# Last rows of a layer norm on VectorE, unread products on TensorE, one column of gelu on ScalarE, and a VectorE step one column later in a recurrence

## The chip, the cores and the metric

One core of a Trainium2 chip runs the whole program in one launch. Its engines are TensorE (matrix products, the profile's PE, with PEld for its weight loads), VectorE (DVE), ScalarE (ACT), GpSimd (POOL) and SyncE (SP), which only issues transfers here. The metric is the device time in microseconds of one execution, lower is better; the median of several executions is compared.

## The reference

A decoder layer of three blocks over x of 2 x 1024 tokens by 256, each followed by a layer norm without weights. All is float32.

```python
# 1 gated linear attention: 16 heads, keys of 8, values of 16; h is 8 x 16 per head
gk = log_sigmoid(x @ Wgk1 @ Wgk2 + bgk2) / 16
h  = h * exp(gt)[..., None] + kt[..., None] * vt[..., None, :]     # 1024 steps
ot = einsum('bhk,bhkv->bhv', qt * scale, h)
o  = o * rsqrt(mean(o * o) + eps) * gnw * (g * sigmoid(g))
x  = layernorm(x + o @ Wo)
# 2 cross attention over 64 of 64 context rows picked by index, 16 heads, latent of 128
x  = layernorm(x + softmax(q k / 4) v @ W_out.T)
# 3 pre-norm causal attention, and 8 gelu experts of 1024, the two best per token
a   = attention(ln(x)) @ Wo + bo + x
mid = gelu(einsum('bsd,edf->bsef', ln2(a), e_w1) + e_b1)
x   = layernorm(x + sum_e w_e * (mid @ e_w2 + e_b2) + a)
```

## The kernel before

The program is written out by hand: each engine has its own list of instructions in each of four program blocks, and semaphores tie them together. There is no scheduler; the order in which a method is called in an engine's function is the order of execution. Tokens are handled in four tiles of 512 (NB = 4), m or k in the code. Between two program blocks all engines meet.

**Block 1, the recurrence** (`front`). The state is kept as 32 columns jj (2 batches x 16 values), each a scan along 1024 steps with 128 rows of head and key. For each column VectorE does `state` (the scan, line 526), perhaps an extra step, `product(jj + 1)` (value times key, line 521) and `output(jj)` (state times query, line 531). TensorE works two columns ahead: `values(jj + 2)` spreads the value row over 128 partitions (line 307), `sums` (line 314) and `turn` (line 320) bring four columns at a time back to tokens. The projections for the second batch are fitted between them: tile 3's x is turned (line 114), ScalarE copies its high part (`x_hi`, line 651), VectorE subtracts it to get the low part (`x_lo`, line 505), TensorE forms the low-rank gate input (`low`, line 263, with Wlp), ScalarE copies it (line 749), TensorE forms the gate (line 273), ScalarE goes through Identity, Abs, Exp and Ln (lines 659 to 667), and VectorE's `log_sigmoid(1)` (line 511) reads it after column 11. ScalarE also makes 0/1 rows for counting indices (`signs`, line 696), which TensorE adds up (line 335).

**Block 2, the cross attention** (`cross_blocks`). It first finishes block 1's output for tiles 2 and 3: product with Wo, statistics on VectorE, and `out_rows` on ScalarE (line 886), which reads y from PSUM (banks G2 = 4, 5 and G3 = 6, 7) and writes normed rows to X. Then for each tile m TensorE runs `exps(m, 0)` (scores again, transposed, lines 1120 and 1124), `c_q` (queries of tile m + 1, line 1005), `values(m, 0)` (lines 1137 and 1140, into banks 6 and 7), `exps(m, 1)`, `scores(m + 1, ...)` (lines 1094 and 1099), `values(m, 1)` and `wout` (line 122). ScalarE takes the exponentials (line 1217), VectorE the maxima (line 1289), the reciprocals of the sums (line 1296) and the quotients (line 1298). `wout` waits for the last quotient.

**Block 3, the causal attention** (`attend`): eight groups g of four heads; TensorE's order goes by steps c of two score banks each; the units of the next group's row maxima (`units`) stand between them, into banks 0 to 3. At c = 16 the maxima are turned. In group 6 (NG - 2) no units follow after c = 14. The last group's order holds the router's first steps: `turn_sums`, `project`, `turn_normed`, `logits`. `warm(n, bank)` (line 1876) issues n products of the identity that nothing reads.

**Block 4, the experts** (`moe`): 256 steps s of one expert's 128 hidden values for 512 tokens. TensorE does a first layer (line 2467) and, three steps later, a second layer (line 2480); ScalarE takes the gelu (line 2549), VectorE splits it in a high and a low part (lines 2614 and 2616). In the first steps expert 0's second-layer weights are also split, the high part on ScalarE (line 2214), the low part on VectorE (line 2219).

## Time and profile before

| | |
|---|---|
| median of three executions | 1375.2 us (1374.62 to 1379.39) |
| the profiled execution | 1377.79 us, of which the span from first to last instruction is 1376.1 us |
| PE busy | 1292.6 us (94% of the span) |
| DVE busy | 978.4 us (71%) |
| ACT busy | 643.9 us (47%) |
| POOL busy | 140.2 us (10%) |
| mean granted TensorE clock | 0.975 of full |

A share of busy time is a mean over four blocks with different limits, so the blocks are read apart. In a list of instructions in order of time, the number ahead of the engine's name is the duration of a group, and the bracket at a row's end is how long the engine sat idle before it and what ended that. A clock of 1.00 is 2.4 GHz and 0.50 is 1.2 GHz. A PE row's duration holds some time of the last product's way through the array, so two neighbouring PE rows overlap a little.

### The profile page before, as it was taken

What the parts mean: (1) busy time and instruction counts of PE and PEld (TensorE: products, weight loads), DVE (VectorE), ACT (ScalarE), POOL (GpSimd) and SP (SyncE); (2) the same over time, 40 slices, a digit from 0 to 9 for tenths busy, and PEclk for the clock granted to TensorE, in tenths of its full rate; (3) what the DMA queues carried; (4) which work ended last, traced back from release to release, by engine and by line L of the source; (5) the groups of instructions that cost most, each with busy time, mean ns of one, the idle gap of its engine ahead of it and who ended that gap; (6) DMA issues with size and microseconds to landing.
All of it is one profiled execution on the core that took longest, in us unless ns stands there. A gap on an engine that the chain in (4) does not pass through costs nothing.

```text
span 1376.1 us, 19007 instructions
## 1 busy us (share of the span) xinstructions
PE 1292.6 (94%) x7577; PEld 954.3 (69%) x7577; DVE 978.4 (71%) x1409; ACT 643.9 (47%) x944; POOL 140.2 (10%) x220
## 2 busy tenths in 40 slices
PE   8786868999899999999999999999999999999997
PEld 7454536567655555557788888888888888888886
DVE  6899996898699898846775655655546556555566
ACT  5677664336468777874433423323223223232233
POOL 5000003000514332210000000000000000000000
PEclk9899989999999999989999999999999999999999
DMA  4000001003522212113000012111101102010001
GB/s 139 1 0 1 0 1 35 1 1 117 171 90 59 64 53 58 55 32 108 16 1 17 4 39 66 48 38 31 57 13 47 39 16 69 16 39 16 1 16 46
DMA packets 40329, 55.78 MB, mean 41 GB/s; under 512 B 9553, under 2 KB 26625, under 8 KB 40241
## 3 DMA queue, kind: packets, MB, share of 16 engines
q1 hardware_dynamic: 35056, 43.67, 10.5%
q0 software_dynamic: 3648, 10.09, 2.6%
q8 instruction: 60, 0.98, 0.3%
q10 hardware_dynamic: 1536, 0.81, 0.2%
q14 instruction: 29, 0.23, 0.1%
HBM read 43.73 MB, written 10.55 MB: 39 GB/s over the span
## 4 chain that ended last, share of the span: by engine, by line
PE 52%; DVE 2%; ACT 1%; issue 0%; ACTq 0%; DVEq 0%
PE PS L2467 25%; PE PS L2480 24%; PE PS L122 1%; PE PS L114 0%; PE PS L2493 0%; PE PS L2228 0%; PE PS L2253 0%; DVE OT_all L2623 0%; DVE r_st L2307 0%; DVE r_on L2324 0%; DVE r_on L2304 0%; PE PS L2505 0%; DVE X L2316 0%; DVE x_mid L2614 0%; ACT X L2586 0%
## 5 line engine op out<-in xcount | busy, mean ns | idle before, releaser
L2549 ACT ACTIVATE x_g<-PS,x_bias 128x512 f32<-128x512 f32 x256 | 175.9, 687 | 494.3 <-PE PS L2467 493.8
L2467 PE MATMUL PS<-x_h,x_w 128*128 128x512 f32 x1536 | 401.1, 396 | 0.5 <-ACT x_g L2549 0.5
L2480 PE MATMUL PS<-x_mid,x_w 128*128 128x512 f32 x1488 | 383.9, 393 | 1.2 <-DVE x_w L2219 1.2
L2467 PEld LDWEIGHTS PS<-x_h,x_w 128*128 128x128 f32 x1536 | 286.9, 188 | 66.1 <-ACT x_g L2549 1.4
L2480 PEld LDWEIGHTS PS<-x_mid,x_w 128*128 128x128 f32 x1488 | 279.2, 188 | 66.0 <-DVE x_w L2219 1.7
L2614 DVE CAST x_mid<-x_g 128x512 fp32r<-128x512 f32 x256 | 109.3, 427 | 275.5 <-ACT x_g L2549 275.3
L2088 DVE TENSOR_REDUCE a_M<-PS 128x2 f32<-128x1024 f32 (+1 forms) x144 | 173.1, 1224 | 26.0 <-PE PS L1792 19.9
L2616 DVE TENSOR_TENSOR x_mid<-x_g,x_mid 128x512 fp32r<-128x512 f32 x256 | 177.2, 692 | 8.8
L2028 ACT ACTIVATE f_parts<-PS 128x512 f32<-128x512 f32 x224 | 120.7, 601 | 36.7 <-PE PS L1846 24.9
L1869 PE MATMUL PS<-f_parts,aV 128*32 128x256 f32 (+1 forms) x960 | 75.9, 398 | 0.2 <-POOL f_parts L1680 0.2
L696 ACT ACTIVATE c_hot<-c_idxT,c_cid 128x1024 bf16<-128x1024 bf16 x65 | 70.7, 1139 | 5.2 <-PE PS L337 3.9
L526 DVE TENSOR_TENSOR_SCAN qh<-decay,qh 128x1024 f32<-128x1024 f32 x32 | 73.0, 2283 | 0.0
L2447 POOL DMA_DIRECT2D x_wb<-route_w x31 | 16.7, 539 | 476.9 <-DVE OT_all L2623 453.2
L1846 PE MATMUL PS<-aQ,aK 64*128 64x512 f32 x192 | 51.0, 488 | 0.7 <-ACT f_h L2028 0.7
L1846 PEld LDWEIGHTS PS<-aQ,aK 64*128 64x128 f32 x192 | 20.4, 184 | 37.8 <-ACT f_parts L2028 27.0
L2623 DVE SCALAR_TENSOR_TENSOR OT_all<-PS,x_bias,x_wb 128x512 f32<-128x512 f32 x62 | 46.2, 745 | 0.0
L1680 POOL TENSOR_SCALAR_AFFINE_SELECT f_parts<-f_parts 128x512 f32<-128x512 f32 x45 | 28.6, 634 | 163.9 <-ACT f_parts L2028 144.4
L307 PE MATMUL PS<-vparts,g_sel 128*128 128x512 f32 x128 | 39.9, 437 | 5.3 <-DVE qh L521 4.6
L1788 PE MATMUL PS<-aK,aQ 64*128 64x512 f32 (+3 forms) x256 | 36.7, 331 | 7.0 <-PEq L1052 2.7
L2219 DVE TENSOR_TENSOR x_w<-x_raw,x_w 128x1024 fp32r<-128x1024 f32 x32 | 38.9, 1219 | 1.4 <-ACT x_w L2214 1.4
L521 DVE TENSOR_TENSOR qh<-PS,KT 128x1024 f32<-128x1024 f32 x32 | 38.6, 1207 | 1.3 <-PE PS L314 1.2
L531 DVE TENSOR_TENSOR qh<-qh,QT 128x1024 f32<-128x1024 f32 x32 | 38.9, 1216 | 0.0
(371 smaller groups left out, 1589.2 us busy)
## 6 DMA issues: line engine op xcount, KB each, us to landing
x_raw<-L_ffn_e_w SPq DMA_DIRECT2D x32, 512.0 KB, 3.8
qk_parts<-f_parts SPq DMA_DIRECT2D x16, 512.0 KB, 3.6
x_wb<-route_w POOLq DMA_DIRECT2D x31, 256.0 KB, 3.4
aQ<-qk_parts SPq DMA_DIRECT2D x96, 64.0 KB, 2.6
aK<-qk_parts SPq DMA_DIRECT2D x60, 64.0 KB, 2.8
X<-x SPq DMA_DIRECT2D x4, 512.0 KB, 7.6
aK<-qk_parts SPq DMA_DIRECT2D x36, 48.0 KB, 2.0
out<-X SPq DMA_DIRECT2D x3, 512.0 KB, 2.9
```

The source lines that it names most:

```text
L526: e.tensor_tensor_scan(qh[:, jj % RQ, :], decay[:, batch(jj // HD)], qh[:, jj % RQ, :], 0.0, ALU.mult, ALU.add).then_inc(s_h, 1)
L696: e.activation(hot[:, n % RS, :], self.idxT[:, :], ACT.Sign, bias=self.cid[:, c:c + 1], scale=2.0).then_inc(s_sg, 1)
L1846: last = e.matmul(bank, K[q][R, s, tile(TB * h if kind == "k0" else kind)], Q[q][R, s, q0:q0 + BLK], start=True, stop=True)
L1869: last = e.matmul(PS[32 * j:32 * j + 32, 7, dst:dst + w], Vs[m % 2][:, kt, j, :], x, start=k in (0, 3) and half == 0, stop=k in (2, NQD - ...
L2028: e.activation(buf[k][:, j, :], PS[:, 4 + b % 3, :], ACT.Exp).then_inc(A.sem, 1)
L2088: e.tensor_reduce(dst, src, AX.X, ALU.max, negate=True).then_inc(VC.sem, 1)
L2467: last = e.matmul(PS[:, f % 2, :], w1[n % 2][u][:, kt, f * P:(f + 1) * P], self.rows(v, k)[:, kt, :], start=m == 0 and kt == 0, stop=m == ...
L2480: last = e.matmul(PS[:, 2 + 2 * (it % 2) + d, :], w2[n % 2][v][:, f, d * P:(d + 1) * P], mid[u][:, f % RM, :], start=f == 0 and m == 0, st ...
L2549: e.activation(g[s % RG][:, :], PS[:, f % 2, :], ACT.Gelu, bias=b1[:, n, f:f + 1]).then_inc(A.sem, 1)
L2614: e.tensor_copy(mid[0][:, f % RM, :], g[s % RG][:, :]).then_inc(V.sem, 1)
L2616: e.tensor_tensor(mid[1][:, f % RM, :], g[s % RG][:, :], mid[0][:, f % RM, :].bitcast(F32), ALU.subtract).then_inc(V.sem, 1)
L2623: e.scalar_tensor_tensor(out=(y if n else sumT[k])[:, d, :], in0=PS[:, 2 + 2 * (it % 2) + d, :], scalar=b2[:, n, d:d + 1], in1=wb[:, it % ...
```

## The change

Five edits.

1. In the recurrence, VectorE's `x_lo(3, 4)` is called after the scan of column 7 instead of column 6.
2. The last normed rows of tile 3 are written by VectorE (`out_rows_vector`: subtract the mean, multiply by the reciprocal deviation) instead of ScalarE (`out_rows`); TensorE's first `values` waits for VectorE's new step "out".
3. In the cross attention, for m = 0, 1 and 2, four products of the identity, 128x512 each, stand ahead of `wout`. Nothing reads them.
4. In the causal attention's group 6, three such products stand at step c = 15 and three at c = 17 (bank 0, behind a wait for the last maximum that reads it), and three more in the last group ahead of `turn_normed`.
5. ScalarE computes the gelu of one column of 128 values behind the router's exponentials, at the end of block 3; nothing reads it.

```diff
@@ recurrence, VectorE @@
                     elif jj == 4:
                         x_lo(2, 4)
-                    elif jj == 6:
+                    elif jj == 7:
                         x_lo(3, 4)
@@ new method @@
+    def out_rows_vector(self, e, m, banks):
+        e.wait_ge(self.OV[m].sem, self.OV[m].at("nmr"))
+        for t in range(TB):
+            last = e.tensor_scalar(self.X[:, m * TB + t, :], self.PS[:, banks[t // 2], t % 2 * D:(t % 2 + 1) * D],
+                                   self.o_mv[m % 2][:, t, 0:1], self.o_rstd[m % 2][:, t:t + 1], ALU.subtract, ALU.mult)
+        last.then_inc(self.OV[m].sem, 1)
@@ cross attention, TensorE @@
-                        e.wait_ge(self.OA[3].sem, self.OA[3].at("out"))
+                        e.wait_ge(self.OV[3].sem, self.OV[3].at("out"))
...
                     scores(m + 1, 3)
+                    for _ in range(4):
+                        e.matmul(PS[:, EB[0], :].rearrange("p (c n) -> p c n", n=P), identr[:, :], identr[:, :].unsqueeze(1).broadcast_to((P, TB, P)), start=True, stop=True)
                     wout(m, range(TB - 1))
@@ cross attention, ScalarE @@
-                self.out_rows(e, 3, G3)
@@ cross attention, VectorE @@
                 self.out_rstd(e, 3)
+                self.out_rows_vector(e, 3, G3)
@@ causal attention, TensorE @@
+                        if g == NG - 2 and c in (15, 17):
+                            e.wait_ge(VC.sem, VC.at(f"c{NU - 2}", NG - 1))
+                            warm(3, SPARE)
...
                 quad_sums(NG - 1, 6)
+                warm(3, SPARE)
                 self.turn_normed(e, 0, FREE)
@@ causal attention, ScalarE @@
                 self.exps(e, 0)
+                e.activation(self.f_nmr[:, 0:1], self.eps[:, 0:1], ACT.Gelu)
                 sums_out(NG - 1, 1)
```

The lines of the changed kernel stand 6 to 16 higher than those of the kernel before. VectorE's order in the recurrence, columns 5 to 8 (minus is before, plus is after; line 505 is `x_lo(3)`):

```order
 L531 TENSOR_TENSOR qh<-qh,QT 128x1024
 L526 SCALAR_TENSOR_TENSOR qh<-decay,qh 128x1024
+L521 TENSOR_TENSOR qh<-PS,KT 128x1024
+L531 TENSOR_TENSOR qh<-qh,QT 128x1024
+L526 SCALAR_TENSOR_TENSOR qh<-decay,qh 128x1024
 L505 TENSOR_TENSOR XTp<-PS,XTp 128x2x512
-L521 TENSOR_TENSOR qh<-PS,KT 128x1024
-L531 TENSOR_TENSOR qh<-qh,QT 128x1024
-L526 SCALAR_TENSOR_TENSOR qh<-decay,qh 128x1024
 L521 TENSOR_TENSOR qh<-PS,KT 128x1024
 L531 TENSOR_TENSOR qh<-qh,QT 128x1024
```

One product, one output and one scan now stand ahead of the low part.

ScalarE's order at the start of the cross attention, before (line 886 is `out_rows`, 1217 the exponentials):

```order
L988 ACTIVATE vparts<-PS 128x512
L886 ACTIVATE X<-PS,go_nmr,go_rstd 128x256 x4
L144 ACTIVATE go_sd<-go_mv,eps 128x4
L886 ACTIVATE X<-PS,go_nmr,go_rstd 128x256 x4
L1217 ACT_TABLE_LOAD
L1217 ACTIVATE pr<-PS 128x512 x4
```

and after:

```order
L994 ACTIVATE vparts<-PS 128x512
L886 ACTIVATE X<-PS,go_nmr,go_rstd 128x256 x4
L144 ACTIVATE go_sd<-go_mv,eps 128x4
L1226 ACT_TABLE_LOAD
L1226 ACTIVATE pr<-PS 128x512 x4
```

The second set of four is gone from ScalarE; it stands on VectorE as `L893 TENSOR_SCALAR`, between the step that ends tile 3's statistics and the split of the queries. The table load now follows the square root.

ScalarE's order from the end of block 3 into block 4, before (line 2276 is the router's exponentials, 2009 the last sums out of PSUM, 2549 the gelu):

```order
L2276 ACTIVATE r_ex<-r_lg 128x32
L2009 ACTIVATE OT_all<-PS 128x512
L1643 UNCONDITIONAL_BRANCH
L2538 UNCONDITIONAL_BRANCH
L2551 ACTIVATE x_bias<-PS 128x80
L2549 ACT_TABLE_LOAD
L2549 ACTIVATE x_g<-PS,x_bias 128x512
```

and after:

```order
L2292 ACTIVATE r_ex<-r_lg 128x32
L2080 ACT_TABLE_LOAD
L2080 ACTIVATE f_nmr<-eps 128x1
L2023 ACTIVATE OT_all<-PS 128x512
L1652 UNCONDITIONAL_BRANCH
L2554 UNCONDITIONAL_BRANCH
L2567 ACTIVATE x_bias<-PS 128x80
L2565 ACTIVATE x_g<-PS,x_bias 128x512
```

The number of table loads stays the same; this one has moved from the front of the first gelu to behind the router's exponentials.

## Rows read from the trace of the kernel before

**Rows 1.** Busy time by stretch: length, then each engine, clock, DMA.

```profile
40.00:206.00 166.00, 125.67 (x708) 76.38 (x707) 158.97 (x138) 122.42 (x129) 0.00 (x0) 0.88 0.00 1
...
629.00:1376.00 747.00, 736.53 (x3332) 602.73 (x3332) 448.18 (x806) 233.61 (x323) 17.71 (x33) 1.00 0.11 34
```

**Rows 2.** Instructions in order of time, recurrence: start, us, engine, line, [idle before].

```profile
60.20 1.23 DVE L505 TENSOR_TENSOR XTp<-PS,XTp 128x1024 fp32r<-128x1024 f32 x1 [3.80 <-ACT XTp L651]
61.35 1.22 DVE L521 TENSOR_TENSOR qh<-PS,KT 128x1024 f32<-128x1024 f32 x1
61.48 2.95 PE L263 MATMUL PS<-XTp,Wlp 128*16 128x512 f32 x12 [1.36 <-DVE XTp L505]
...
65.27 1.00 ACT L749 ACTIVATE c_L<-PS 16x1024 f32<-16x1024 f32 x1
65.81 1.20 DVE L521 TENSOR_TENSOR qh<-PS,KT 128x1024 f32<-128x1024 f32 x1
...
66.32 1.98 PE L273 MATMUL PS<-c_L,Wgk 16*128 16x512 f32 x4 [0.20 <-ACT c_L L749]
```

**Rows 3.** The same, where VectorE meets ScalarE again.

```profile
82.38 1.06 ACT L667 ACTIVATE decay<-decay 128x1024 f32<-128x1024 f32 x1
83.60 1.20 DVE L511 SCALAR_TENSOR_TENSOR z<-z,decay 128x1024 f32<-128x1024 f32 x1
89.61 1.22 DVE L514 TENSOR_TENSOR vparts<-PS,vparts 128x1024 fp32r<-128x1024 f32 x1 [0.34 <-ACT vparts L681]
```

**Rows 4.** The same, start of the cross attention.

```profile
233.21 0.30 ACT L144 ACTIVATE go_sd<-go_mv,eps 128x4 f32<-128x4 f32 x1 [4.07 <-DVE go_mv L139]
233.95 1.93 ACT L886 ACTIVATE X<-PS,go_nmr,go_rstd 128x256 f32<-128x256 f32 x4 [0.45 <-DVE go_nmr L880]
233.97 2.89 PE L1005 MATMUL PS<-vparts,Wgp 128*128 128x512 f32 x12
235.90 1.28 ACT L1217 ACT_TABLE_LOAD   x1
236.90 0.69 DVE L1015 TENSOR_SCALAR qT_hi<-PS 128x512 fp32r<-128x512 f32 x1 [2.98 <-PE PS L1005]
237.20 2.06 ACT L1217 ACTIVATE pr<-PS 128x512 f32<-128x512 f32 x4
239.31 1.63 PE L1137 MATMUL PS<-pr,c_Vblk 128*32 128x512 f32 x8 [2.45 <-ACT pr L1217]
242.58 1.20 PE L1120 MATMUL PS<-vparts,XTp 32*128 32x512 f32 x12
```

**Rows 5.** Busy time in one microsecond of it.

```profile
241.00:242.00 1.00, 1.00 (x8) 0.00 (x0) 0.00 (x0) 0.00 (x0) 0.00 (x0) 0.50 0.00 0
```

**Rows 6.** The same two steps of TensorE for the next tile.

```profile
265.70 1.06 PE L1137 MATMUL PS<-pr,c_Vblk 128*32 128x512 f32 x8
...
267.55 0.74 PE L1120 MATMUL PS<-qT_hi,XTp 32*128 32x512 f32 x8
```

**Rows 7.** TensorE ahead of `wout`, in order of time.

```profile
255.02 2.86 PE L122 MATMUL PS<-c_WoutT,c_Kblk 128*128 128x256 f32 x12 [1.08 <-DVE c_Kblk L1298]
```

**Rows 8.** Line 492's fourteen unread products.

```profile
L492 PE MATMUL PS<-c_idr x14: 388/389/389, 203.3 to 206.3; 128*128 128x512 f32 x14
```

**Rows 9.** One microsecond near the end of the causal attention.

```profile
617.00:618.00 1.00, 1.00 (x2) 0.32 (x2) 0.00 (x0) 0.55 (x1) 0.00 (x0) 0.50 0.00 0
```

**Rows 10.** TensorE's idle time where products are added.

```profile
585.14 0.49 PE L1846 MATMUL PS<-aQ,aK 64*128 64x512 f32 x2 [0.67 <-ACT f_h L2028]
...
606.60 1.09 PE L114 MATMUL PS<-ident,r_on 128*128 128x128 f32 x8 [0.88 <-DVE r_on L2324]
```

**Rows 11.** From the causal attention's end into the experts.

```profile
616.95 0.60 ACT L2009 ACTIVATE OT_all<-PS 128x512 f32<-128x512 f32 x1 [2.80 <-PE PS L1869]
...
622.07 1.28 ACT L2549 ACT_TABLE_LOAD   x1 [2.49 <-PE PS L2467]
...
628.98 1.66 PE L2480 MATMUL PS<-x_mid,x_w 128*128 128x512 f32 x6 [1.22 <-DVE x_w L2219]
```

More of the change, by code:

```diff
@@ L822, in out_buffers @@
         self.OA = [self.steps(f"go_act{m}", ["sq", "sqrt", "ogT", "sd", "out"]) for m in range(NB)]
-        self.OV = [self.steps(f"go_dve{m}", ["ms", "rs", "norm", "gate", *self.NORM, "nmr"]) for m in range(NB)]
+        self.OV = [self.steps(f"go_dve{m}", ["ms", "rs", "norm", "gate", *self.NORM, "nmr", "out"]) for m in range(NB)]
         self.og, self.ogT = {}, {}
```

## The prediction

> **What bounds the kernel now.** I read the chain of waits first (nearly all of it is TensorE's two expert layers), then busy time by stretch, then each place that an edit touches in the list of instructions in order of time, looking at two things in a row: the bracket at its end (who was waited for) and the start against the end of the row it needs. Three limits follow one another. In the recurrence VectorE is busy 159.0 of 166.0 us [rows 1], so a wait of VectorE there looks like lost time. In the cross attention the engines hand work to each other and whatever releases TensorE's next step counts. In the experts TensorE is busy 736.5 of 747.0 us [rows 1]; there only what TensorE waits for at the very start can still be won, and everything won earlier is kept, since no later stretch waits for a fixed time.
>
> **Edit 1, the low part a column later.** VectorE idles 3.80 us ahead of `x_lo(3)`, until ScalarE has copied the high part [rows 2]. It was free at 60.20 - 3.80 = 56.40. Now a whole column goes first; from product to product a column takes 65.81 - 61.35 = 4.46 us, so the low part starts at 60.86 at the earliest, when its input is long there, and the 3.8 us of idling become work. That would be 3.80 us if VectorE stayed the limit. Two things speak against it. First, the low part itself comes 60.86 - 60.20 = 0.66 us later, and TensorE's `low` (61.48) was waiting for just it. ScalarE takes the result at 65.27 with nothing idle ahead of it, while `low` ended at about 64.4, so ScalarE does not notice; TensorE does, for its gate product at 66.32 had only 0.20 us of idle time ahead of it [rows 2]. The chain behind it is therefore late by 0.66 - 0.20 = 0.46 us at most, and by about 0.2 if the modelled end of the product before it is generous; I take 0.3. Second, VectorE needs this chain again: the Ln that `log_sigmoid(1)` reads ends at 82.38 + 1.06 = 83.44, and VectorE takes it at 83.60; the values' high part is waited for at 89.61 with 0.34 us idle [rows 3]. So VectorE had only 0.16 us of slack at 83.60 although it had lost 3.80 us before, and it can't come earlier than ScalarE. What it wins at 60 it waits at 83.6. Cost: +0.3 us; bounds +0.5 and, if the chain moved with VectorE after all, -3.8.
>
> **Edit 2, tile 3's rows.** ScalarE writes them from 233.95 to 235.88, loads the exponential's table (1.28 us) and exponentiates from 237.20 to 239.26; TensorE idles 2.45 us and starts `values` at 239.31, 0.05 behind [rows 4]. Without the rows ScalarE goes from the square root's end, 233.21 + 0.30 = 233.51, to the load, and is through with the exponentials at 233.51 + 0.02 + 1.28 + 2.06 = 236.87. TensorE's query product ends at 233.97 + 2.89 = 236.86, so `values` starts at 236.92: 2.39 us earlier. VectorE has the cover: it idles 2.98 us up to 236.90 [rows 4]. The trace has no such step on 256 columns out of PSUM; the nearest row is line 1015's on 512 columns, 0.69 us. Four steps cost between 4 x 0.35 and 4 x 0.69, 1.4 to 2.8 us, and end between 235.4 and 236.8 when started at 233.95: hidden at both ends, barely so at the upper. I take half the width, half the price. What is late next is TensorE's own query product.
>
> The idle 2.45 us had a second price. The granted clock behind it is 0.50, that is 1.2 GHz [rows 5], and from `values` to the next step (1137 to 1120) pass 242.58 - 239.31 = 3.27 us; for the next tile at full clock 267.55 - 265.70 = 1.85 us [rows 4, 6]. With the gap gone TensorE is busy throughout and I take the clock to stay at 2.4 GHz: another 1.4 us. TensorE stands idle next only ahead of `wout` (1.08 us, waiting for the quotient) [rows 7], and VectorE's reciprocals, which feed that, start on the end of `values`; so both parts arrive. Sum -3.8 us; bounds -2.4 (the clock falls anyway) and -4.1.
>
> **Edit 3, unread products ahead of `wout`.** Fourteen of the same form start between 203.3 and 206.3, (206.3 - 203.3) / 13 = 0.23 us each [rows 8]; four are 0.92 us against 1.08 us of idle time [rows 7]. They run instead of a wait: 0. At half clock they would be 1.84 us and cost 0.76 us, three times. The clock at these places is full now, so they also win nothing. 0, bounds 0 and +2.3.
>
> **Edit 4, nine more.** Three are 0.7 us. Ahead of `turn_normed` TensorE idles 0.88 us, hidden. Those at c = 17 stand before the last group's first scores; TensorE idles 0.67 us a little later, at 585.14 [rows 10], which takes them up at full clock; at half clock they are 1.4 us and cost 0.7. Those at c = 15 fall in a wait for ScalarE. If they keep the clock up that otherwise falls, as much comes back. 0, bounds -1.0 and +0.7.
>
> **Edit 5, gelu's table.** The load at 622.07 stands between TensorE's first layer and the first gelu. The second layer's first product, at 628.98, waited 1.22 us for the split of expert 0's weights on VectorE [rows 11], and the split waits for ScalarE, which does gelu, copy, gelu, copy in turn behind that load. So 1.28 us of load are 1.28 us of this chain. Ahead of 628.98 the second product of weights and both gelus only wait for ScalarE or have their products by then, so the whole comes through, and behind it TensorE is the limit. The new place is free: ScalarE idles 2.80 us ahead of 616.95 [rows 11], and load and one column are 1.28 + 0.25 us. -1.3 us; bounds 0 (a load that is still needed) and -1.5.
>
> The Trainium skill ("ScalarE: Activation LUTs", What ACT_TABLE_LOAD costs) gives such a switch 1.28 us and another 1.38 us for a drain, 2.66 us together. By that edit 5 would bring 2.7 us, and in edit 2 the exponentials would end later. The trace disagrees: from the load's start at 235.90 to the first exponential at 237.20 pass 1.30 us [rows 4].
>
> **The sum.** +0.3 - 3.8 + 0 + 0 - 1.3 = -4.8 us. The profiled execution took 1377.79 us, 1376.1 of span and 1.7 around it: 1373.0 us. It lies 2.6 us above the median 1375.2, and since the edits' terms don't depend on that, I take them from the median: 1370.4 us.
>
> **Rivals.** (a) VectorE is the limit of the recurrence after all, because the chain through ScalarE moves forward too: -3.8 instead of +0.3, so 1366.3 us. For it: 159.0 of 166.0 us busy [rows 1]. Against it: the slack of 0.16 us at 83.60 and the wait at 89.61 [rows 3]; the chain's next input from VectorE is the low part, and that comes later. (b) The unread products keep TensorE's clock up where it is 0.50 now, at the causal attention's end and the experts' start [rows 9]. Each microsecond at half clock in which TensorE is the limit gives back 0.5; were it 6 us of that kind (a guess at its length), 3 us, 1367.4 us. Against it: at 617 the clock is low, and the nearest added products stand ahead of 606.60, ten microseconds earlier, and fill only 0.7 us. (c) Slower: the first `values` now waits for VectorE's four steps. They decide from (236.87 - 233.95) / 4 = 0.73 us each; the whole change turns slower once they delay `values` past 239.31 by more than edits 5 and 1 leave, 1.0 us, that is from (239.26 + 1.0 - 233.95) / 4 = 1.6 us each. At 2.0 us each: 233.95 + 8.0 = 241.95, +2.7 us, less 1.0, so 1376.9 us. Against it: 0.69 us for twice the columns [rows 4]. (d) The clock falls at the same place all the same: 1.4 us less, 1371.8 us, and if the added products then run at half clock too, up to 3 us less, 1374.8 us.
>
> The Trainium skill ("TensorE: Matmul & The Clock Gate", Part 1) says that where the clock rises or falls varies from run to run of one kernel with the moment at which its products begin. No run here shows that yet; it would make (b) and (d) a matter of the run as much as of the change.
>
> **How the numbers follow.** Forecast 0.62; (a) 0.12; (b) 0.08; (c) 0.03; (d) 0.15. The forecast alone has 1369 to 1372 us. The range takes in (a) in part and the first half of (d): 1367.0 to 1373.8 us. What a measurement of this kernel tells from no change is 0.5%, 6.9 us, so faster is below 1368.3 us: (a), (b) and a little of the forecast, 0.20. Slower is above 1382.1 us: (c) at its far end, 0.03. The rest 0.77.
>
> **What would show it.** Edit 1: no idle time ahead of line 505, and instead two to four microseconds ahead of lines 521 and 511 between 75 and 84 us, with 511 at 83.7 to 84.0. Edit 2: `values` 0.1 us behind the query product, about 236.9, and a clock of 1.00 up to `exps`. Edit 3: no idle time left ahead of `wout`, and its start still on the quotient. Edit 5: no load at the first gelu, and the second layer's first product 5.6 us after ScalarE turns to the first gelu, where before it came 628.98 - 622.07 = 6.9 us after. I am wrong if VectorE enters column 12 over 1 us earlier than before, if the four steps end later than the exponentials, or if the experts' first second-layer product starts less than 1 us earlier against their first product.

## The result, and the profile after

| | before | after |
|---|---|---|
| median of the first comparison, us | 1375.35 (1374.18 to 1379.39, 6 runs) | 1367.91 (1365.43 to 1368.77, 6 runs) |
| ratio, 95% interval | | 0.9936 [0.9919, 0.9953] |
| ratio when measured again (f1 below) | | 0.9959 [0.9943, 0.9974] |
| mean of the runs that come with a clock, both sessions, us | 1374.88 (82 runs) | 1368.09 (12 runs) |
| mean granted clock of these runs | 0.9783 | 0.9810 |
| profiled execution, span, us | 1377.79, 1376.1 | 1367.98, 1366.2 |

The forecast was 1370.4 us, with no change beyond 0.5% as the likeliest outcome. The first ratio is 0.64% below one and clear of its uncertainty; over both sessions the means differ by 6.8 us, 0.49%. The gain is real and larger than the 4.8 us that the prediction summed, although the median of 1367.91 us lies inside its range of 1367.0 to 1373.8 us.

The profiled run of before lies 2.9 us above the mean of its kernel, that of after 0.1 us below it. So the 9.9 us between the two spans are more than the change brings, and the difference has to be split by place before any of it is credited to an edit. Busy time by stretch of the kernel after (length, then PE, PEld, DVE, ACT, POOL, granted clock, DMA share, GB/s):

```profile
40.00:206.00 166.00, 124.11 (x695) 73.88 (x694) 157.82 (x137) 122.58 (x129) 0.00 (x0) 0.88 0.00 1
629.00:1366.00 737.00, 726.70 (x3283) 594.46 (x3281) 440.30 (x792) 230.37 (x319) 17.22 (x32) 1.00 0.11 32
...
241.00:242.00 1.00, 1.00 (x5) 0.81 (x5) 1.00 (x1) 0.46 (x1) 0.00 (x0) 1.00 0.00 0
617.00:618.00 1.00, 1.00 (x5) 0.49 (x3) 0.96 (x3) 0.70 (x2) 0.57 (x1) 1.00 0.21 29
...
64.00:66.00 2.00, 2.00 (x6) 0.71 (x5) 2.00 (x3) 1.93 (x2) 0.00 (x0) 0.50 0.01 4
...
606.00:609.00 3.00, 3.00 (x22) 1.27 (x20) 1.97 (x12) 2.43 (x4) 0.83 (x2) 0.50 0.02 5
```

The same limits hold as in [rows 1]: VectorE in the recurrence, TensorE in the experts. The microseconds at 241 and 617, both at 0.50 before [rows 5, 9], are now at 1.00, that is 2.4 GHz. At 241 no stretch at half clock is left near. At 617 the comparison flatters: the change has moved the same work some 7 us earlier, and there 606 to 609 us is at 0.50. Before, half clock lasted from 611.7 to 622.0 us; now it lasts from 606.0 to 609.4 us. It is shorter, not gone.

The start of the cross attention after the change, in order of time, answers to [rows 4, 7]:

```profile
234.28 0.30 ACT L144 ACTIVATE go_sd<-go_mv,eps 128x4 f32<-128x4 f32 x1 [4.07 <-DVE go_mv L139]
234.60 1.28 ACT L1226 ACT_TABLE_LOAD   x1
235.03 1.90 DVE L893 TENSOR_SCALAR X<-PS,go_mv,go_rstd 128x256 f32<-128x256 f32 x4
235.90 2.06 ACT L1226 ACTIVATE pr<-PS 128x512 f32<-128x512 f32 x4
238.01 1.06 PE L1143 MATMUL PS<-pr,c_Vblk 128*32 128x512 f32 x8
239.87 0.97 PE L1126 MATMUL PS<-vparts,XTp 32*128 32x512 f32 x12
...
250.84 1.09 PE L1180 MATMUL PS<-c_idr 128*128 128x512 f32 x4
252.09 1.13 PE L122 MATMUL PS<-c_WoutT,c_Kblk 128*128 128x256 f32 x4 [0.16 <-DVE c_Kblk L1306]
```

The four rows on VectorE take 1.90 us together and end at 236.93, before the exponentials at 237.96. `values` (L1143) has no idle time ahead of it, and from it to the next step pass 239.87 - 238.01 = 1.86 us, against 3.27 before. From tile 3's square root to the output projection pass 252.09 - 234.28 = 17.81 us; before it was 255.02 - 233.21 = 21.81. That is edit 2, 4.0 us. The root itself comes 1.07 us later.

Further on, four rows of the kernel before (first units of the causal attention, turn of its first group, turn of its last, first product of the experts):

```profile
348.98 0.79 PE L1788 MATMUL PS<-aK,aQ 64*128 64x512 f32 x2 [2.73 <-PEq L1052]
...
386.53 0.67 PE L1817 MATMUL PS<-a_idr,a_nmp 128*128 128x128 f32 x5
...
579.91 0.77 PE L1817 MATMUL PS<-a_idr,a_nmp 128*128 128x128 f32 x5
...
618.93 0.37 PE L2507 MATMUL PS<-ident,r_eb 80*128 80x80 f32 x1 [0.90 <-PEq L1643]
```

And the same four of the kernel after, with ScalarE's gelu table and the second layer's first product, which answer to [rows 11]:

```profile
346.06 0.50 PE L1797 MATMUL PS<-aK,aQ 64*128 64x512 f32 x2 [2.70 <-PEq L1058]
...
382.12 1.00 PE L1826 MATMUL PS<-a_idr,a_nmp 128*128 128x128 f32 x8
...
574.50 1.11 PE L1826 MATMUL PS<-a_idr,a_nmp 128*128 128x128 f32 x8
...
607.77 1.28 ACT L2080 ACT_TABLE_LOAD   x1
609.07 0.20 ACT L2080 ACTIVATE f_nmr<-eps 128x1 f32<-128x1 f32 x1
...
611.62 0.26 PE L2523 MATMUL PS<-ident,r_eb 80*128 80x80 f32 x1 [0.91 <-PEq L1652]
...
619.12 1.66 PE L2496 MATMUL PS<-x_mid,x_w 128*128 128x512 f32 x6 [1.12 <-DVE x_w L2235]
```

Each pair gives one line of a ledger; the last column is what that stretch alone gained.

| reached | before | after | difference | of this stretch |
|---|---|---|---|---|
| tile 3's square root | 233.21 | 234.28 | +1.07 | +1.07 |
| first output projection | 255.02 | 252.09 | -2.93 | -4.00 |
| first units, causal attention | 348.98 | 346.06 | -2.92 | 0 |
| turn of its first group | 386.53 | 382.12 | -4.41 | -1.49 |
| turn of its last group | 579.91 | 574.50 | -5.41 | -1.00 |
| experts' first product | 618.93 | 611.62 | -7.31 | -1.90 |
| second layer's first product | 628.98 | 619.12 | -9.86 | -2.55 |
| end of the span | 1376.1 | 1366.2 | -9.9 | 0 |

Two of these were forecast (-4.0, and half of -2.55), and of the +1.07 the forecast had +0.3. The lines -1.49, -1.00, -1.90 and the other half of -2.55 were not forecast, and none of them has an instruction that went away. They are the matter of the experiments.

### The profile page after: what moved, and what is told of

Its sections match the earlier page's. It is cut to its first block, busy times and chain, and to the rows that moved or that the text cites. A ratio compares the mean times of both kernels' runs of the same rounds, so it can differ in the third digit from the quotient of the medians.

```text
span 1366.2 us, 19050 instructions
## 1 busy us (share of the span) xinstructions
PE 1289.1 (94%) x7598; PEld 952.8 (70%) x7598; DVE 981.6 (72%) x1413; ACT 642.6 (47%) x941; POOL 139.8 (10%) x220
## 4 chain that ended last, share of the span: by engine, by line
PE 52%; DVE 2%; ACT 0%; issue 0%; ACTq 0%; DVEq 0%
PE PS L2483 25%; PE PS L2496 24%; PE PS L122 1%; PE PS L114 0%; PE PS L2509 0%; PE PS L2244 0%; PE PS L2269 0%; DVE OT_all L2639 0%; DVE r_st L2323 0%; DVE r_on L2340 0%; DVE r_on L2320 0%; PE PS L2521 0%; DVE X L2332 0%; DVE x_mid L2630 0%; ACT X L2602 0%
```

## The experiments

Every kernel was compared with the kernel before on the same chip. The table has also, from each kernel's one profiled execution, four stretches in us: A, from tile 3's square root to the first output projection; B, from the first group product of the fused projections (L1471) inside cross attention to the causal attention's first turn; C, from its last turn to the experts' first product, and D, from there to the second layer's first product.

| kernel | median us (runs) | ratio, 95% | mean clock | A | B | C | D |
|---|---|---|---|---|---|---|---|
| before | 1374.9 (82) | | 0.9783 | 21.81 | 68.21 | 39.02 | 10.05 |
| after (all five) | 1367.9 (6) | 0.9936 [0.9919, 0.9953] | 0.9820 | 17.81 | 66.73 | 37.12 | 7.50 |
| e1: edit 1 | 1374.37 (12) | 0.9996 [0.9984, 1.0008] | 0.9785 | 21.80 | 68.34 | 36.94 | 8.79 |
| e2: edit 2 | 1369.85 (7) | 0.9956 [0.9940, 0.9973] | 0.9803 | 17.80 | 66.70 | 37.08 | 8.77 |
| e3: edit 4 | 1372.56 (12) | 0.9980 [0.9969, 0.9992] | 0.9802 | 21.80 | 68.20 | 35.99 | 8.78 |
| e4: edit 5 | 1373.04 (12) | 0.9980 [0.9968, 0.9992] | 0.9785 | 21.79 | 68.28 | 39.09 | 8.76 |
| f1: all five | 1368.13 (6) | 0.9959 [0.9943, 0.9974] | 0.9800 | 17.79 | 66.69 | 36.09 | 7.51 |
| f2: all but 1 | 1366.26 (5) | 0.9939 [0.9925, 0.9954] | 0.9818 | 17.78 | 66.71 | 37.18 | 7.50 |
| f3: all but 4 | 1367.46 (5) | 0.9957 [0.9942, 0.9971] | 0.9798 | 17.79 | 66.70 | 37.99 | 7.50 |
| f4: all but 3 | 1368.08 (5) | 0.9950 [0.9937, 0.9964] | 0.9816 | 17.78 | 66.64 | 36.02 | 7.50 |
| g1: 2 and 5 | 1368.39 (7) | 0.9959 [0.9943, 0.9975] | 0.9796 | 17.75 | 68.13 | 36.04 | 7.51 |
| g2: f2, 8 more | 1364.13 (5) | 0.9923 [0.9911, 0.9935] | 0.9844 | 17.75 | 65.60 | 37.20 | 7.51 |
| g3: pause filled | 1372.07 (12) | 0.9983 [0.9972, 0.9993] | 0.9795 | 20.19 | 66.72 | 37.93 | 8.79 |
| g4: last three of 4 | 1373.80 (11) | 0.9994 [0.9985, 1.0002] | 0.9790 | 21.79 | 68.21 | 37.91 | 8.78 |
| h1: 1 doubled | 1383.04 (6) | 1.0065 [1.0050, 1.0080] | 0.9750 | 21.79 | 68.16 | 37.79 | 8.78 |
| h2: first six of 4 | 1372.52 (11) | 0.9991 [0.9981, 1.0000] | 0.9798 | 21.81 | 68.20 | 35.98 | 8.76 |
| h3: g2, 8 more | 1366.22 (5) | 0.9944 [0.9931, 0.9958] | 0.9844 | 17.81 | 65.44 | 37.09 | 7.48 |

From the second layer's first product to the end every kernel takes 747.1 us (747.08 to 747.14), so what is won or lost ahead of it reaches the end whole.

A straight line through all these runs (time against mean granted clock, one slope for all kernels, each with its own height) has 0.85 us for each 0.001 of clock, with 0.9 us of scatter left. By its heights the kernels stand to before, at the same clock, as follows: all five -4.5 (+-0.6), e1 -0.1 (+-0.6), e2 -3.7 (+-0.7), e3 -0.5 (+-0.6), e4 -1.4 (+-0.6), g1 -5.0 (+-0.7), f2 -5.7 (+-0.9). This is a rough split, because a microsecond at half clock doesn't cost the same everywhere (the last section has its price by stretch), but it shows which kernels differ by more than their clock.

**e1 to e4: one edit at a time.** e1:

```diff
-                    elif jj == 6:
+                    elif jj == 7:
                         x_lo(3, 4)
```

> The kernel before with edit 1 alone (the low part a column later). Theory 1 (VectorE's idle time before the low part is slack that the chain through TensorE and ScalarE takes back at column 11): between +0.2 and +1.1 us, with idle time of VectorE in front of the product of column 7 to 10 and of log_sigmoid. Rival (VectorE is the limit): -3 to -3.8 us.

e2 (with the vector helper and the wait on it):

```diff
-                self.out_rows(e, 3, G3)                  # scalar
+                self.out_rows_vector(e, 3, G3)           # vector, behind out_rstd(e, 3)
```

> The kernel before with edit 2 alone (tile 3's last normed rows on VectorE). Theory 1: 2.4 us of idle time and 1.4 to 1.7 us of half clock go, -3.8 to -4.1 us. Rival (the half clock after the gap is a matter of the run, and comes up elsewhere): -2.4 us.

e3:

```diff
+                        if g == NG - 2 and c in (15, 17):
+                            e.wait_ge(VC.sem, VC.at(f"c{NU - 2}", NG - 1))
+                            warm(3, SPARE)
...
+                warm(3, SPARE)
                 self.turn_normed(e, 0, FREE)
```

> The kernel before with edit 4 alone (nine unread products at the end of the causal attention). Theory 2 (they keep the clock at 2.4 GHz there and at the front of the experts): -2 to -3.5 us, and the half-clock stretches near 581 and 612 us gone or shorter. Rival (what the changed kernel's trace shows there is a matter of the run's phase): 0, within 0.7 us.

e4:

```diff
                 self.exps(e, 0)
+                e.activation(self.f_nmr[:, 0:1], self.eps[:, 0:1], ACT.Gelu)
```

> The kernel before with edit 5 alone (one column of gelu at the end of the causal attention). Theory 1: the table load leaves the chain to the first second-layer product, -1.3 us. Rival (a table switch costs a load and a drain): -2.7 us. Rival (it was hidden): 0.

Measured, ratios turned into time on 1375 us: -0.6, -6.1, -2.8 and -2.8 us. Edit 2 takes A from 21.81 to 17.80 as forecast, and B by 1.5 us besides, with no product added anywhere. Edit 5 has D at 8.76, but so have e1 to e3 without it, and its D holds time at half clock, which theirs does not. Its -2.8 us looks like the rival's -2.7 (a load and a drain), but at an equal clock it is -1.4, and its own stretch moves by the load alone. The clean comparison is by kernels whose clock is full in D: 8.76 to 8.79 without the edit (e1, e2, e3, g3, g4, h1, h2), 7.48 to 7.51 with it (after, f1 to f4, g1, g2, h3). Edit 5 is 1.3 us. Edit 4, which removes nothing, is faster by 0.2% [0.08%, 0.31%], mostly by a clock higher by 0.0019. The forecast had it at nothing.

**f1 to f4: all five again, and one left out at a time.** The edits are those above, and for f4

```diff
-                    for _ in range(4):
-                        e.matmul(PS[:, EB[0], :]..., identr, identr, ...)
                     wout(m, range(TB - 1))
```

> All five edits again, beside the kernels that leave one out. The four single edits measured so far were worth -0.6, -6.1, -2.8 and -2.8 us against before, in sum -12.2. Theory (clock): at an equal mean granted clock the edits are worth the -4.8 us of the written sum, and the rest is half-clock time that goes, which can go only once: the whole stays near -8.8, ratio 0.9936, between 1366 and 1369 us, clock 0.981 to 0.982. Rival (the parts add): -12.2 us, ratio 0.991, 1363 to 1365 us.

> All but edit 1 (the low part of tile 3's inputs stays in its earlier column). Theory (edit 1 costs what the first ledger showed, the square root of tile 3 at 234.28 against 233.21 us): this kernel is 1 us faster than all five, ratio 0.9929 if they have 0.9936, with the square root of tile 3 before 233.3 us. Rival (edit 1 is worth the -0.6 us that its own run had, or nothing): ratio equal to or up to 0.0004 above that of all five.

> All but edit 4 (the nine unread products at the end of causal attention). Theory (the nine products take half-clock time away at the experts' front): 2 to 3 us slower than all five, ratio 0.9951 to 0.9958, with the mean granted clock down by 0.001 to 0.002 and a half-clock stretch of several us near 605 to 612 us. Rival (edits 2 and 5 alone take that half-clock time away, since they shorten the pauses): within 0.5 us of all five, ratio 0.9936 to 0.994.

> All but edit 3 (the four unread products ahead of each output projection of cross attention, which has no run of its own yet). Theory: they lie in TensorE's idle time and keep no clock up there, so the time is that of all five within 0.5 us and the first units of causal attention come as late. Rival one: they hold the clock up at the change from cross to causal attention (half-clock stretch of 3.4 us there with them, 6.8 without in the profiled before), and leaving them out costs 1 to 1.5 us. Rival two: TensorE is late behind them and leaving them out gains 1 to 3 us.

All five gave -5.6 us this time, with an interval of 2 us on either side, which leaves out the single edits' sum of -12.2. By means over all runs the two are nearer, -9.5 against -6.8. Without edit 1 the median was 1.9 us lower (1366.26 against 1368.13), but the intervals of the two ratios overlap. Without edit 4 the kernel was no slower by its median and had the clock of f1 (0.9798 against 0.9800), so the expected 2 to 3 us did not come; C is 37.99 against 36.09 in the one profiled execution of each. Without edit 3 nothing changed that could be measured (0.9950 against 0.9959). Its A is 17.78 in place of 17.79, its B 66.64 in place of 66.69: edit 3 is nothing, and rival one, that it holds the clock up ahead of causal attention, falls.

The full clock in C has to be read with care. In f1 and f4 a stretch at half clock stands further ahead, among the groups (491 to 494 us in f1, 411 to 415 us in f4), and their groups take 194.0 and 193.7 us, the longest of the seventeen. What C saved there was in part paid before it.

**g1: edits 2 and 5 alone.**

> Edits 2 and 5 alone. Alone they measured -6.1 and -2.8 us; at an equal granted clock (0.98) the pooled runs give -4.0 and -1.6. Theory (edits 2 and 5 are all that saves work; edits 1, 3 and 4 only move the clock or cost): -5.6 us at equal clock and, with the clock of edit 2, 1.5 to 2.5 more, 1367 to 1368.5 us, ratio 0.994 to 0.995, at least as fast as all five in the same conditions. Rival (edit 4 is needed for the clock at the experts' front): 2 to 3 us slower than all but edit 1 (0.9939), ratio 0.996, mean granted clock 0.979 or less.

0.9959 with a wide spread (1364.81 to 1374.11), and a clock of 0.9796 against 0.9818 for the same with edits 3 and 4 (f2). That is the rival's number for the ratio. The clock is that of f3, which also lacks edit 4 (0.9798). But its profiled execution has C at 36.04, with a full clock all through, so edit 4 is not needed for that in each execution; and its B is 68.13 although edit 2 is in. Both stretches are thus a matter of the execution as well as of the kernel. The microseconds 570 to 625 of this kernel, with the columns as above, against the same of before:

```profile
570.00:625.00 55.00, 49.73 (x407) 32.30 (x405) 33.74 (x68) 41.08 (x70) 9.40 (x15) 1.00 0.16 50
```

```profile
570.00:625.00 55.00, 51.51 (x435) 29.97 (x431) 29.10 (x55) 40.49 (x72) 8.32 (x13) 0.88 0.07 20
```

**g3: the pause filled, the rows left on ScalarE.**

```diff
                 def values(m, g):
+                    if m == 0 and g == 0:
+                        e.wait_ge(self.OA[3].sem, self.OA[3].at("out"))
+                        for _ in range(9):
+                            e.matmul(PS[:, 6, :]..., identr, identr, ...)
                     e.wait_ge(A2.sem, A2.at(f"p{4 * g + 3}", m))
```

> The kernel before, with nine unread products on TensorE in the pause of 2.45 us ahead of the first values of cross attention (236.9 to 239.3 us), and ScalarE's rows of tile 3 left where they are. It pays the pause in full and takes only the half clock away. Theory (edit 2's 4.0 us at the output projection are 2.6 of pause and 1.4 of half clock, and a half-clock stretch of 3.4 us at the start of causal attention goes with it): the stretch near 240 us is gone, the first output projection comes 1.2 to 1.5 us nearer to the square root of tile 3 (20.4 in place of 21.8 us after it), and the whole gains 1.2 to 3 us, ratio 0.998 to 0.999. Rival (the half clock comes for another reason than the pause, or the products push the values back): the stretch stays, or 21.8 us or more from the square root to the projection, ratio 1.000 or more.

```profile
235.26 2.20 PE L1132 MATMUL PS<-c_idr 128*128 128x512 f32 x9
237.90 1.06 PE L1141 MATMUL PS<-pr,c_Vblk 128*32 128x512 f32 x8 [0.43 <-ACT pr L1221]
...
239.75 0.97 PE L1120 MATMUL PS<-vparts,XTp 32*128 32x512 f32 x12
...
251.98 1.35 PE L122 MATMUL PS<-c_WoutT,c_Kblk 128*128 128x256 f32 x5 [1.09 <-DVE c_Kblk L1302]
```

The nine products take the place of 2.0 of the 2.45 us in which TensorE stood idle, `values` still waits for ScalarE, and from it to the next step pass 1.85 us instead of 3.27. A is 20.19: of edit 2's 4.0 us, 1.6 are clock and 2.4 the pause itself, which is the prediction's split (1.4 and 2.4) to 0.2 us. B fell too, from 68.2 to 66.72, though nothing in B was touched, and the whole gained 2.3 us [1.0, 3.9]. So what comes with edit 2 in B comes from a TensorE without its pause at 237 us, not from the rows on VectorE. That rests on one execution of g3, and on B standing at 68.2 to 68.3 us in all seven kernels that keep the pause. Why what TensorE does at 237 us decides how long it runs at half clock after 346 us, I can't show.

**g2: eight more products at the end of cross attention.**

```diff
                 e.wait_ge(V3.sem, V3.at("y", m))
-                for _ in range(8):
+                for _ in range(16):
                     e.matmul(PS[:, 6, :]..., identr, identr, ...)
```

> All but edit 1, and the row of 8 unread products at the end of cross attention made 16. TensorE stood idle for 2.7 us there in every trace and a half-clock stretch followed in every one. Theory (the idle time ahead of causal attention brings that stretch): the stretch near 345 us is gone and the first units of causal attention to the first turn of group 0 take 0.7 to 1.5 us less; 0.5 to 1.5 us faster than all but edit 1, ratio 0.993. Rival (the products push the block's end out, since TensorE is the last there): the first unit comes up to 2 us later than in all but edit 1 and the time is that of all but edit 1 or up to 1.5 us more.

The first units of the causal attention and the eight microseconds around them, without the eight (f2):

```profile
345.05 0.50 PE L1796 MATMUL PS<-aK,aQ 64*128 64x512 f32 x2 [2.69 <-PEq L1058]
```

```profile
344.00:352.00 8.00, 6.95 (x41) 5.59 (x42) 4.12 (x4) 3.29 (x6) 7.57 (x8) 0.79 0.38 100
```

and with them:

```profile
339.82 3.90 PE L1208 MATMUL PS<-c_idr 128*128 128x512 f32 x16
345.01 0.50 PE L1796 MATMUL PS<-aK,aQ 64*128 64x512 f32 x2 [1.29 <-issue]
```

```profile
344.00:352.00 8.00, 6.99 (x47) 5.69 (x48) 5.70 (x5) 3.34 (x6) 7.70 (x8) 1.00 0.46 128
```

The idle time ahead of the first unit halves, the clock stays at 1.00 where it was 0.79, and B falls by another 1.1 us (65.44 in h3, which has the same row of 16). The rival is right in a small part: from the output projection to the first unit this kernel takes 0.4 us more (345.01 - 250.69 against 345.05 - 251.14). It is the fastest kernel of the study, 0.9923 against the 0.9939 of f2 (their intervals overlap) and the 0.9936 and 0.9959 of all five.

**g4 and h2: edit 4 in two parts.** g4 keeps only the three products ahead of `turn_normed`, h2 only the six in columns 15 and 17.

> Of edit 4 only its last three unread products, those ahead of the turn of the normed rows near 601 us. Theory (they fill the idle time ahead of the half-clock stretch at the experts' front): no half-clock stretch between 600 and 625 us, from the last turn to the experts' first product 36 to 37.2 us in place of 39.0, mean granted clock 0.979 to 0.980, ratio 0.998 to 0.999. Rival (it is the six products in columns 15 and 17 that count): the stretch of 6.8 to 10.2 us near 611 us stays and the ratio is 0.9995 to 1.0005.

> Of edit 4 only the six unread products in columns 15 and 17 of the last group but one. All nine alone gave 0.998, the last three alone 0.9994 with a mean granted clock of 0.979. Theory (the parts of edit 4 share its 0.0020 of clock, the six having the larger part): ratio 0.9985 to 0.999, mean granted clock 0.979 to 0.980. Rival (only all nine together keep the clock up, or the gain of the nine was spread of the runs): ratio 0.9995 to 1.0005, clock 0.978.

-0.8 us [-2.1, 0.3] and -1.2 us [-2.6, 0]: each less than the nine, both on the border of what can be told from nothing. C is 37.91 with the three and 35.98, at full clock throughout, with the six. In g4 the clock is 1.00 from 600 to 625 us, as its theory had it, but 0.52 from 581 to 588 us, so C didn't fall to the expected 36 to 37.2 us: the half clock stood at another place. Taken over the profiled executions: with the nine or the six, C has 36.0 to 37.2 us (seven kernels, mean 36.5), with neither 36.0 to 39.1 (eight, mean 37.7); g4 stands with the latter. The difference of 1.2 us has an uncertainty of 0.9; with the groups ahead counted in, it is 1.0 with an uncertainty of 1.2. One execution of each can't do more than suggest that the six count for more.

**h3: more of them at the front.**

```diff
-                warm(3, SPARE)
+                warm(5, SPARE)
                 self.turn_normed(e, 0, FREE)
...
-                warm(2, SPARE)
+                warm(5, SPARE)
                 quad_sums(NG - 1, 9)
-                warm(2, SPARE)
+                warm(5, SPARE)
```

> The fastest so far (all but edit 1, 16 products at the end of cross attention) with 5 unread products in place of 3 ahead of the turn of the normed rows and 5 in place of 2 in each of the two rows at the end of causal attention: 8 more, 1.8 us of TensorE at 0.23 us each. TensorE's idle time from 600 to 610.5 us is 0.2 and 0.9 us there. Theory (idle time there brings the half-clock stretch near 605 us): no stretch there, and last turn to the experts' first product 36 to 36.8 us in place of 37.2; ratio 0.9915 to 0.9923. Rival (the products are in the way, since TensorE has less idle time than they take): that stretch of the ledger is 37.5 us or more, ratio 0.993 to 0.994.

```profile
570.00:625.00 55.00, 52.09 (x412) 34.49 (x409) 33.02 (x67) 40.23 (x69) 9.39 (x15) 1.00 0.16 49
```

Both theories got something: the clock stays at 1.00, where g2 had half clock near 605 us, and C is 37.09 all the same, 0.1 us less than with the half clock and 1.0 to 1.1 more than the 36.0 us of kernels at full clock with fewer products. The eight cost what they save there, and the median is 2.1 us above that of g2 (0.9944 against 0.9923, the intervals just overlap) at the same mean clock. A high clock can be paid for at more than it is worth.

**h1: the low part two columns later.**

```diff
-                    elif jj == 6:
+                    elif jj == 8:
                         x_lo(3, 4)
```

> Before, with the low part of tile 3's inputs two columns later in the recurrence (column 8) where edit 1 puts it one later (7). Theory (edit 1 costs 1.3 us, since the mean time of tile 3's square root is 233.8 us over the five profiled kernels with it and 232.5 over the nine without): 1.5 to 3 us slower than before, ratio 1.001 to 1.002, square root near 234 to 236 us. Rival (the piece only moves where VectorE's idle time lies, and the difference is spread of the runs): ratio 0.9992 to 1.0005, square root between 231.2 and 233.6 us.

The recurrence of the kernel after (VectorE and what it waits for), which answers to [rows 2, 3]:

```profile
57.25 1.23 DVE L521 TENSOR_TENSOR qh<-PS,KT 128x1024 f32<-128x1024 f32 x1 [1.22 <-PE PS L307]
...
61.72 1.20 DVE L505 TENSOR_TENSOR XTp<-PS,XTp 128x1024 fp32r<-128x1024 f32 x1
...
62.98 4.51 PE L263 MATMUL PS<-XTp,Wlp 128*16 128x512 f32 x12 [2.28 <-DVE XTp L505]
...
67.52 1.01 ACT L749 ACTIVATE c_L<-PS 16x1024 f32<-16x1024 f32 x1 [1.59 <-PE PS L263]
...
69.19 1.22 DVE L521 TENSOR_TENSOR qh<-PS,KT 128x1024 f32<-128x1024 f32 x1 [1.80 <-PE PS L307]
...
84.52 1.23 DVE L511 SCALAR_TENSOR_TENSOR z<-z,decay 128x1024 f32<-128x1024 f32 x1 [0.78 <-ACT decay L667]
...
90.64 1.23 DVE L514 TENSOR_TENSOR vparts<-PS,vparts 128x1024 fp32r<-128x1024 f32 x1 [0.43 <-ACT vparts L681]
```

and of h1:

```profile
66.33 1.20 DVE L505 TENSOR_TENSOR XTp<-PS,XTp 128x1024 fp32r<-128x1024 f32 x1
67.58 4.17 PE L263 MATMUL PS<-XTp,Wlp 128*16 128x512 f32 x12 [6.76 <-DVE XTp L505]
...
73.46 1.22 DVE L521 TENSOR_TENSOR qh<-PS,KT 128x1024 f32<-128x1024 f32 x1 [5.93 <-PE PS L307]
```

8.9 us slower [6.9, 11.0], several times what either theory had; the square root comes at 241.03. TensorE issues in its written order, so behind L263 it can't start the column's products; it stands idle 6.76 us for the low part, runs L263 in 4.17 us (2.95 before [rows 2]), and only then makes what VectorE has waited 5.93 us for. In the kernel after the same is seen small: 2.28 us idle, L263 in 4.51 us, VectorE waiting 1.80. So the cost of this delay is not proportional. One column later is about where the slack ends.

The longer L263 is the clock again. In the eleven kernels without the edit it takes 2.95 or 2.96 us, at a clock of 1.00, and TensorE idles 1.4 us ahead of it. In the five kernels with edit 1 TensorE idles 2.1 to 3.1 us ahead of it, and it takes 4.3 to 5.3 us at a clock of 0.50 to 0.65. The longest is that of e1:

```profile
61.67 5.30 PE L263 MATMUL PS<-XTp,Wlp 128*16 128x512 f32 x12 [2.82 <-DVE XTp L505]
```

## Why the prediction was wrong

**The step that failed** is the tacit assumption, in the sum, that the clock behind 242 us stays as it was. It stands in two terms: edit 2's sum was closed at the output projection, and edit 4, the unread products, was put at "0, bounds -1.0 and +0.7". In its place the runs showed -1.5 us or more in B whenever TensorE's pause at 237 us was gone or filled (all but one of ten executions), and -1.2 us in C with the nine or six products, the weaker of the two: leaving edit 4 out of all five (f3) cost nothing that could be measured. Rival (b) named the clock (3 us, 1367.4 us, close to what came) and was given 0.08. That its number came close is in part luck. The larger piece, B, is not where it looked, and comes in e2 without any added product. For C, its reason against, the ten microseconds between products and half clock, is not what decided: in h2 and h3 the clock is full up to the experts' second layer with all added products issued by 607 us, and in g1 it is full with none of the nine.

By the stretches of all profiled executions the change comes to this. Edit 2: -4.0 (A, the same to 0.1 us in nine kernels with it against seven without; g3 apart). B: -1.5 in six of nine kernels with edit 2 and in g3 (-2.6 to -2.8 in g2 and h3, nothing in g1). C: -1.2, the difference of the two means above. Edit 5: -1.3 (D). Edit 1: +1.1 in the profiled pair. Sum -6.9 us, against 6.8 measured over all runs; that they agree to 0.1 us is chance, since C alone is uncertain by 0.9 and edit 1 by over 1. The forecast had -3.8, 0, 0, -1.3 and +0.3. The missing 2.1 us are 2.7 us of clock in B and C less 0.8 on edit 1, and 0.2 on edit 2. The other 3 us of the profiled pair are an execution of before that ran longer at half clock in C and D than most (1.9 us of them), and 1.0 us in the groups between, a stretch of 191.9 to 194.0 us over the seventeen profiled executions, without a pattern by edits.

**Edit 2 was right in each part:** pause 2.4 us, clock 1.6 instead of 1.4 (g3), the four steps 1.90 us between the bounds 1.4 and 2.8 (0.48 us each, between 0.35 and 0.69), and they end 1.0 us ahead of the exponentials. `values` then follows the query product, which was named as next. What I left out is B.

**Edit 5 was right** to 0.1 us: the load stands in idle time at 607.77, and the experts' front is shorter by its length. From ScalarE's first gelu, which starts at 613.50, to the second layer's first product at 619.12 pass 5.6 us, as forecast. From the load's start at 607.77 to the row behind it at 609.07 pass 1.30 us, as before.

**Edit 3 was right at 0** (f4). Its four products take up 0.92 us of the 1.08 idle, and 0.16 us of waiting for the quotient are left.

**Edit 1 had the right mechanism, and a term was left out.** The mechanism is seen: no idle time ahead of L505, and instead 1.80, 0.99 and 0.78 us ahead of 521 and 511. The sum took `low` (L263) to run as before, only 0.66 us later. It started 1.5 us later, since in this execution VectorE waited 1.22 us at 57.25 first (as in f4 and h1 alone besides), and it took 4.51 us, at half clock for most of it (the row 64 to 66 us above), where it had taken 2.95. All five kernels with the edit show this longer L263. So L511 came at 84.52 where I had put it at 83.7 to 84.0; over the profiled kernels it starts at 82.9 to 84.5 us with the edit (mean 84.0) and at 82.0 to 83.7 without (mean 83.1).

What that is worth at the end stays open. Tile 3's square root comes at 232.2 to 234.9 us (five with edit 1, mean 233.8) and at 231.2 to 233.6 (eleven without, mean 232.6), 1.3 us later with about 1.3 of uncertainty. Part of this spread is not the edit's: of the eleven, the four with a clock of 0.92 from 36 to 57 us (e2, e4, g1, g3) have the root at 231.2 to 231.9 and the seven with 0.76 have it at 232.65 to 233.6. Among kernels with 0.76 there, the three with the edit are 0.9 us later. All five against all but edit 1 points the same way (1.9 us by the medians, 1.2 at equal clock). Yet alone, over twelve runs, the edit costs nothing (-0.6 +-1.7 us).

Rival (a), a gain of 3.8 us, is refuted by all of them. Rival (c) is refuted by 1.90 us, and (d) by the clock of 1.00 at 241.

## What to carry to other kernels

When a wait of TensorE is taken away or filled, price the clock as well as the wait, and not only at that place: look at each later stretch at 0.50 in the profile as something that may go. Products whose result no one reads were worth their time here only inside idle time of TensorE: eight ahead of a stretch at half clock brought 1.1 us where TensorE idled 2.7 us, and eight where it idled under 1 us cost as much as they saved. Where one profiled execution stands 3 us off its kernel's mean, compare stretches over many kernels that share the code, since single pairs credit the spread to the edit.

## What the runs showed of the hardware that was not expected

The execution time of one kernel follows its mean granted clock: before ran between 1370.8 and 1379.7 us, at clocks of 0.975 to 0.982, and 0.001 of clock goes with 0.85 us. The same kernels' stretch C took 36.0 us at full clock and 39.0 in before, where about 10.5 us of it were at half clock, so a microsecond at half clock cost 0.3 us there, not the 0.5 that it would if TensorE were the limit throughout. Ahead of `wout` it cost 0.47 (3.4 us at half clock, 1.6 us of time), and in the first 38 us of the causal attention 0.44 (37.5, 36.0 and 34.5 us with 6.8, 3.4 and 0 us at half clock).

The recurrence is not free of it either. About 40 us of it are at half clock (0.88 over 166 us [rows 1]) although VectorE is busy nearly throughout. From 36 to 57 us the clock was 0.92 in four of the eleven profiled kernels without edit 1 and 0.76 in seven, 6.7 us more at half clock, and tile 3's square root came 1.6 us later in the seven (mean 233.1 against 231.6): 0.24 us for each. VectorE's idle time ahead of L505 was 2.7 to 3.0 us in the four and 3.6 to 3.9 in the seven, so more than half of it is seen to reach VectorE there.

Filling a pause near 237 us, or taking it away, went with less time at half clock behind 346 us in nine of ten executions (3.4 us or none, where the tenth, g1, has 6.3 and the seven kernels with the pause 6.6 to 6.8). The traces don't say by what.
